# The conversion of h2 to bf16, moved from one block of 32 DMAs into the first pass's w1/w2 loop

## The reference

```
xn = layernorm(x)                          # x: 4 x 4096 x 1024
# attention-like branch
magnitude = sigmoid(xn @ W_mag.T + b_mag) * 5
mem_r, mem_i = cumsum(magnitude*xn*cos(phi)), cumsum(magnitude*xn*sin(phi))
context = concat(xn*cos, xn*sin, retrieved_r, retrieved_i)     # 4096 wide
h = gelu(layernorm(context) @ W1.T + b1)   # 4096 -> 2048
attn = xn + h @ W2.T + b2                  # 2048 -> 1024
# FFN branch, weights are -1, 0 or 1
f = silu(xn @ w1.T * w1_s) * (xn @ w2.T * w2_s)   # 1024 -> 4096, twice
f = gelu(f @ h1.T * h1_s)                  # 4096 -> 4096
f = gelu(f @ h2.T * h2_s)                  # 4096 -> 4096
ffn = f @ w3.T * w3_s                      # 4096 -> 1024
out = x + attn + ffn
```

## Time and profile before

| | us |
|---|---|
| median of 2 runs | 5136.91 (5087.21 to 5186.61) |
| the profiled execution | 4832.19 |
| its span, slowest core (core 5) | 4830.6 |
| spans of the 8 cores | 4803.4 to 4830.6 |

### The profile page before, as it was taken

The page is one execution under the profiler, slowest core; times in us unless marked ns, Lnnn a source line. Parts: engine busy times, 40 slices in busy tenths (PEclk is TensorE's granted clock), DMA queues, the critical chain, the costliest instruction groups (busy, mean ns, idle before and its releaser), DMA issues.

```text
span 4830.6 us, 45973 instructions; the slowest of 8 cores (4803.4 to 4830.6 us)
## 1 busy us (share of the span) xinstructions
PE 3565.3 (74%) x15504; PEld 1546.7 (32%) x15504; DVE 1547.7 (32%) x3659; ACT 804.6 (17%) x1129; POOL 399.9 (8%) x756
## 2 busy tenths in 40 slices
PE   3335011328879999888798998887989987899993
PEld 3211000013324344333343443333434433344441
DVE  2342888630127540211374402113743020100003
ACT  2111102200123311001234100012331000110100
POOL 0002001000210000002100000020000000200000
PEclk9987555569989899899898999998979999999997
DMA  2247999986764334668542346785424466844443
GB/s 76 74 111 133 109 116 112 109 108 120 117 124 148 113 122 150 124 132 125 126 148 105 131 148 125 134 127 125 155 87 148 144 127 122 127 147 153 148 143 79
DMA packets 125695, 600.84 MB, mean 124 GB/s; under 512 B 15867, under 2 KB 15900, under 8 KB 78364
## 3 DMA queue, kind: packets, MB, share of 16 engines
q0 software_dynamic: 108288, 545.31, 53.9%
q1 hardware_dynamic: 17180, 52.60, 3.4%
HBM read 866.29 MB, written 75.50 MB: 195 GB/s over the span
## 4 chain that ended last, share of the span: by engine, by line
PE 58%; DMA 20%; DVE 13%; issue 7%; ACT 1%; DVEq 1%; SPq 0%; POOLq 0%; ACTq 0%
PE ps L507 46%; DMA wstage<-w_t 10%; DMA wstage<-fw_t 5%; PE ps L1102 3%; PE ps L1093 2%; PE ps L820 1%; PE ps L999 1%; PE ps L989 1%; DMA xo<-x_fm 1%; DVE xo L475 1%; DMA wstage<-wmag_t 1%; DMA xo<-xp_fm 1%; PE ps L333 1%; PE ps L398 1%; ACT big L390 1%
## 5 line engine op out<-in xcount | busy, mean ns | idle before, releaser
L507 PE MATMUL ps<-big,wstage 128*128 128x512 bf16 x12032 | 2713.2, 388 | 394.7 <-DMA wstage<-w_t 182.5
L507 PEld LDWEIGHTS ps<-big,wstage 128*128 128x128 bf16 x12032 | 1189.3, 100 | 1921.9 <-issue 587.6
L1184 DVE SCALAR_TENSOR_TENSOR obuf<-ps,svv_s,obuf 128x512 f32<-128x512 f32 x32 | 24.0, 751 | 1214.2 <-PE ps L507 1214.2
L1112 DVE SCALAR_TENSOR_TENSOR big<-ps,svv_s,big 128x512 bf16<-128x512 f32 x128 | 96.1, 751 | 965.0 <-PE ps L1102 965.0
L820 PE MATMUL ps<-xn_hi,wstage 128*128 128x512 bf16 x512 | 125.7, 410 | 318.9 <-DVE big L701 224.2
L1102 PE MATMUL ps<-xn_hi,wstage 128*128 128x512 bf16 x1024 | 244.0, 381 | 38.1 <-DMA wstage<-fw_t 35.1
L1093 PE MATMUL ps<-xn_hi,wstage 128*128 128x512 bf16 x1024 | 242.6, 380 | 28.5 <-DMA wstage<-fw_t 21.9
L1165 ACT ACTIVATE big<-ps,svv_h2s 128x512 bf16<-128x512 f32 x128 | 88.2, 689 | 778.8 <-PE ps L507 778.8
L999 PE MATMUL ps<-big,sel_b_sb 128*33 128x512 bf16 x128 | 73.6, 575 | 172.7 <-ACT big L995 143.2
L820 PEld LDWEIGHTS ps<-xn_hi,wstage 128*128 128x128 bf16 x512 | 52.5, 104 | 392.1 <-issue 341.8
L228 POOL DMA_DIRECT2D wstage<-w_t x128 | 68.2, 532 | 1286.1 <-PE ps L507 1212.1
(11 more groups left out here) (158 smaller groups left out, 2199.3 us busy)
## 6 DMA issues: line engine op xcount, KB each, us to landing
wstage<-h1b POOLq DMA_DIRECT2D x128, 1024.0 KB, 5.1
wstage<-h2b POOLq DMA_DIRECT2D x128, 1024.0 KB, 5.1
wstage<-w_t POOLq DMA_DIRECT2D x96, 1024.0 KB, 9.2
wstage<-fw_t POOLq DMA_DIRECT2D x256, 256.0 KB, 5.0
h1b<-h_t POOLq DMA_DIRECT2D x32, 1024.0 KB, 69.7
h2b<-h_t POOLq DMA_DIRECT2D x32, 1024.0 KB, 163.2
xo<-x_fm SPq DMA_DIRECT2D x48, 512.0 KB, 5.5
xo<-xp_fm SPq DMA_DIRECT2D x32, 512.0 KB, 3.5
```

Of the source, the lines that this page charges most:

```text
L507: last = e.matmul(psum[bank][:, 0:NMOV], wt_ap, mov_fn(k), start=(k == 0), stop=(k == K - 1))
L1112: V(lambda e, m=m, bankB=bankB, yb=yb, ctxb=ctxb: e.scalar_tensor_tensor(out=big2[:, yb + m * M:yb + (m + 1) * M], in0=psum[bankB][:, 0:NM ...
```

## The change

The block of 32 h2 conversions that stood behind `emit_A1(0)` is gone. Instead, in pass 0, each of the 32 steps of the w1/w2 loop issues its own one, on the same GpSimd queue, right behind the step's two weight loads. After the loop the count of the conversions' semaphore is recorded in `B_CVH2`, so that the h2b loads wait for all 32, as before. The number and the form of the DMAs are the same; the other engines' lists are the same.

```diff
     emit_A1(0)
-    emit_convert(dr["h2b"], dr["h2_t"], DH, 0, 32, B_CVH2, "CV2")
+    h2ch = []
+    for _m in range(32):
+        def _c2(_m=_m):
+            dop("gpsimd", "CV2",
+                ap3(dr["h2b"], _m * 128 * DH, [[1, 1], [1, 128 * DH]]),
+                ap3(dr["h2_t"], _m * 128 * DH, [[1, 1], [1, 128 * DH]]))
+        h2ch.append(_c2)
     for _s in emit_mid(0, alt=True):
         _s()
...
             dop("gpsimd", f"LDW{slotB}", apB, wslice_ap(dr["fw2_t"], m, D, DH),
                 writes=[B_WS4[slotB]])
+            if pm == 0:
+                h2ch[m]()
...
+
+        if pm == 0:
+            B_CVH2.w = {"CV2": cnt["CV2"]}
 
         if pm + 1 < NP:
             emit_A0(pm + 1)
```

## The result

The changed kernel is slower: the ratio to the kernel before is 1.0513, with a 95% interval of 1.048 to 1.0546. The profiled execution took 5068.19 us where that of before took 4832.19 us, +236 us; the sum had said +242 us for it. The time that was written down, 5379 us, was carried to a median of 5136.91 us over the two runs then shown. With eight more runs the median of before is 4839.46 us (4826.86 to 5187.28). The median of the changed kernel over its 11 runs is 5368.56 us (5068.19 to 5453.59; a twelfth execution, outside this count, took 5120.80 us).

The account below looks back on a forecast made before the run. The prediction took full DMA engines and VectorE's chain to bound the stretch before W1, and DMA the changed loop. Its terms, -31 + 273 = +242 us, gave 5074 us from the profiled execution, 5379 us from the median; range 5040 to 5440 us.

Parts of the forecast that it names:

- the sum: Whole kernel: -31 us ahead of W1 and +273 us in the w1/w2 loop make +242 us.
- Removed, -31 us: Ahead of the attention's w1 projection: without the block, PE starts when VectorE ends, 30.85 us less; nothing else gained there.
- One period, 13.0 us: Each step of the w1/w2 loop lasts the DMA time of one conversion and one pair of loads, 13.0 us.
- The two rates per piece added: Step of the w1/w2 loop: conversion at 9.6 us plus load pair at 3.5 us gives 13.1 us.
- the third way: Step of the w1/w2 loop: counting reads, conversion plus loads at 328 GB/s take 12.8 us.
- The stage, 407 us: w1/w2 loop of pass 0: 31 periods of 13.0 us plus 4 us of PE, 407 us against 134 us, +273 us.
- The last conversion, counted as 0: Behind the w1/w2 loop: its 9.6 us lie in PE's 27.45 us wait for VectorE; 5 us at most, counted as 0.
- What would show it: Profile signs: W1 starts at VectorE's end; loop waits some 9 us per step, DMA share 0.99 or more; later stages only shifted.
- carried to it, the sum is 5379 us: Final step: the median shown lay 305 us above the profiled execution, so 5074 us was given as 5379 us.
- the first two rivals: FFN to h1 stages: loads pass conversions; either conversions fit idle DMA time, 4801 us, chance 0.05, or +106 us, chance 0.04.
- The cheaper conversion between loads: w1/w2 loop: a conversion costs less when alternating with loads, +109 to +200 us in all; chance 0.12.
- the dearer one: w1/w2 loop: each period pays the latencies again, as in the 15.47 us pattern, +290 to +320 us; chance 0.08.

Follow-up runs that it names:

- the copy: Changed kernel, but each of the 32 DMAs copies 1 MB of bf16 h1b to h2b instead of converting h2; 4962.77 us, +131 us.
- the last run: Kernel before, with 16 h1 conversions paced by VectorE's statistics chunks, 16 h1 and 4 h2 behind the wmag loads, 28 h2 in the old place; ratio 0.9878.

## Why the prediction was right or wrong

*Direction, mechanism and size of the difference: right.* Each step, by its term:

- Removed, -31 us: in the mean of the eight cores PE starts W1 31.0 us earlier (31.5 on core 5), right behind VectorE, and the w1/w2 loop 30.7 us earlier. So nothing else was gained there, which was also predicted.
- One period, 13.0 us: measured 12.69 us, or 12.79 without the last two steps, which were shorter. The two rates per piece added (9.6 + 3.5 = 13.1) were slightly too high; the third way, bytes in both directions at 328 GB/s, gave 12.8 and is the one that the copy confirms (9.5 us expected, 9.49 measured). I took a value between the ways.
- The stage, 407 us: on core 6 from 1215.30 to 1618.7 us, 403 us; in the mean of all cores 401 us against 131 us, +270 us. The last conversion, counted as 0, did nearly hide in VectorE's wait: on cores 1, 3, 5 and 6 PE idles there for 28.0 to 28.3 us, within 1 us of before, on the other four for 30.3 to 31.3 us, 2 to 4 us longer than before.
- The sum, +242 us: in the mean of the eight cores the next A1 stage starts 240.6 us later, and the spans are 234.8 us longer. The profiled executions differ by 236 us, and the ratio makes +248.
- What would show it: the DMA share of 1.00 and 123 GB/s (120 said), the chain through the fw_t loads, and an unchanged h1 stage came out. The wait of PE before each step is 6.8 us in the mean (9 said; at half the clock PE itself fills more of the step). The first h2b load did not have to wait for the conversions: on core 6 it is issued at 1894.2 us, 243.7 us later than before, as all of that stretch.

*The step that failed is the last one of the sum*, "carried to it, the sum is 5379 us": the 305 us added there are no time of the kernel. The median of two runs, 5136.91 us, rested on two executions that the comparison leaves out. The other seven of before lie at 4826.86 to 4850.88 us, beside the 4832.19 us of the profiled execution. I saw that the two stood 305 us apart and took the one that the heading of the times named. So 5379 us is 294 us above the 5085.4 us measured, while the sum at the profiled execution's own level, 5074 us, is 11 us below it, and 6 us above the 5068.19 us of the profiled one. That the median over all 11 runs, 5368.56 us, comes near 5379 is chance: it hangs on how many of the longer runs happened to be among the 11. That the 242 us hold on either level, which the prediction assumed, no trace shows, and the range of 5040 to 5440 us was wide enough for both, so it tested nothing between them.

The chance of slower and the first two rivals were sound: loads pass no conversion on their own queue (21.0 us to landing, 312.30 us behind a full block). The cheaper conversion between loads (+109 to +200 us) fell with the share of 1.00; the dearer one (15.5 us a period) with the 12.69 us.

## What to carry to other kernels

A background transfer costs by where it stands, not by how long it takes: some 290 us of conversions beside a chain of VectorE cost nothing, and the same bytes ahead of weight loads that PE waits for cost 270 us of their 307, all but the DMA time that lay idle there and the last conversion, which fell into a wait for VectorE. Before such a block is moved, compare its DMA time (here 307 us) with the idle DMA time of the new place (20 us), not with the 31 us of stall at its end; that stall was to be had by moving four of the 32. Idle DMA time early in the program can be used, but paced, or the block takes it from SyncE's queue too.

## What the runs showed that I had not expected

- *A deep backlog on GpSimd's queue holds up SyncE's DMAs.* With 22 conversions queued, the eleventh small transfer of SyncE's took 10.9 us to issue and the five behind it 24 to 31 us each, instead of some 0.4 us, and the two x_fm loads issued in that time landed after 60.6 us (median) instead of 3.5. The Trainium skill, "DMA: Bandwidth & Descriptors", Queues, rings and completion order, says that the engines take turns between queues packet by packet; the trace shows that SyncE does get through within the backlog, but one small transfer at a time, each in the time of two and a half to three conversions. Why a turn takes that long, no run shows. With one conversion for every two chunks, x_fm loads took 6.2 us and the statistics kept their pace: on core 1 of the last run PE's last matmuls of them start at 299.6 us, against 300.3 us before.
- *PE's clock follows its gaps.* In the changed loop the groups behind a wait of 6 to 8 us run at 3.57 us and the mean granted clock is 0.71; in the kernel with the block behind the loop the same groups take 1.89 us at 1.00. The lower clock set no pace, as PE had finished before the next loads came, and the loss was the same in both kernels.
